# Two residual blocks, deformable stage: VectorE makes four of the nine products of hats per pair, GpSimd keeps five

## What is computed

```python
out = relu(group_norm(conv(x, w1), ...))                 # 1024 -> 256 channels, 1x1
om = conv(out, w_off, pad=1) + b_off                     # 27 channels: 9 x-offsets, 9 y-offsets, 9 masks
off_x, off_y, mask = om[:, :9], om[:, 9:18], sigmoid(om[:, 18:])
py, px = grid_y + ky + off_y, grid_x + kx + off_x        # a place for every pixel and tap
sampled = bilinear_sample(out, py, px) * mask            # 9 taps per pixel
out = einsum('bckhw,ock->bohw', sampled, w2)             # the deformed 3x3 convolution, 256 -> 256
out = relu(group_norm(out, ...))
out = group_norm(conv(out, w3), ...)                     # 256 -> 1024, 1x1
return relu(out + x)
```

## Time and profile before

| | us |
|---|---|
| median of 3 runs | 2977.31 |
| lowest and highest of them | 2972.14, 2982.18 |
| the profiled execution's own time | 2978.64 |
| its span, first to last instruction | 2976.6 |
| PE busy | 2915.8 (98%) |
| DVE busy | 2397.4 (81%) |
| ACT busy | 1795.9 (60%) |
| POOL busy | 712.0 (24%) |

### The profile page before, as it was taken

How to read it: one execution, slowest core, us unless ns; L and a number is a source line. 1 busy time by engine, 2 the same in 40 slices (tenths; PEclk the granted TensorE clock), 3 DMA queues, 4 the chain that set the end, 5 groups by cost and what they waited for, 6 DMA issues and landing times.

```text
span 2976.6 us, 46528 instructions
## 1 busy us (share of the span) xinstructions
PE 2915.8 (98%) x16518; PEld 2864.6 (96%) x16518; DVE 2397.4 (81%) x4872; ACT 1795.9 (60%) x3281; POOL 712.0 (24%) x433
## 2 busy tenths in 40 slices
PE   9999999999998999999999999999999999999997
PEld 9999999999997899999999999999999999999997
DVE  5655888965666688898888988888888888889885
ACT  5544322346664566676666666676776667666664
POOL 0000000000001333333333333333333333333331
PEclk9999999999999999999999999999999999999998
DMA  7774111035653344444444444544444444454431
GB/s 270 218 234 131 44 44 44 22 128 201 262 225 114 122 151 154 152 144 153 152 154 151 143 156 145 163 147 146 159 145 162 146 147 156 149 158 149 147 119 73
DMA packets 209207, 437.39 MB, mean 147 GB/s; under 512 B 18640, under 2 KB 170192, under 8 KB 203344
## 3 DMA queue, kind: packets, MB, share of 16 engines
q1 hardware_dynamic: 159408, 326.82, 32.6%
q10 hardware_dynamic: 49568, 107.60, 11.1%
HBM read 307.71 MB, written 126.64 MB: 146 GB/s over the span
## 4 chain that ended last, share of the span: by engine, by line
PE 56%; DVE 10%; ACT 1%; issue 0%; DMA 0%; POOL 0%; ACTq 0%; SPq 0%; DVEq 0%; POOLq 0%
PE sample L86 6%; PE sample L91 6%; PE deform L86 6%; PE deform L91 6%; PE sample L87 6%; PE deform L87 6%; PE work L86 5%; PE work L91 5%; PE work L87 5%; DVE s_lo L1805 3%; DVE x L1829 2%; DVE x L1711 1%; DVE x_lo L1717 1%; DVE v_lo L1813 1%; PE work L73 1%; PE work L75 1%
## 5 line engine op out<-in xcount | busy, mean ns | idle before, releaser
L1667 POOL TENSOR_TENSOR hats<-hats 98x784 f32<-98x784 f32 x288 | 597.6, 2075 | 909.8 <-DMA hats<-hat_scratch 888.9
L1459 ACT ACTIVATE v_hi<-sample 128x392 fp32r<-128x392 f32 (+1 forms) x640 | 292.2, 463 | 322.5 <-PE sample L91 312.7
L86 PE MATMUL sample<-s_hi,aT_hi 98*128 98x392 f32 (+1 forms) x1280 | 418.1, 332 | 6.4 <-DVE v_lo L1813 6.1
L87 PE MATMUL sample<-s_hi,aT_lo 98*128 98x392 f32 (+1 forms) x1280 | 412.7, 328 | 0.0
L86 PE MATMUL deform<-v_hi,w_w 128*128 128x392 f32 x1152 | 403.7, 350 | 0.0
L87 PE MATMUL deform<-v_hi,w_w 128*128 128x392 f32 x1152 | 393.2, 341 | 0.0
L1813 DVE TENSOR_TENSOR v_lo<-sample,v_hi 128x392 fp32r<-128x392 f32 (+1 forms) x640 | 326.4, 517 | 71.1 <-ACT v_hi L1459 69.9
L1805 DVE TENSOR_TENSOR s_lo<-hats,s_hi 98x784 fp32r<-98x784 f32 x288 | 360.1, 1251 | 2.7 <-ACT s_hi L1450 1.7
L91 PE MATMUL sample<-s_lo,aT_hi 98*128 98x392 f32 (+1 forms) x1280 | 316.4, 328 | 7.1 <-DVE s_lo L1805 7.1
L91 PE MATMUL deform<-v_lo,w_w 128*128 128x392 f32 x1152 | 310.7, 342 | 0.0
L1450 ACT ACTIVATE s_hi<-hats 98x784 fp32r<-98x784 f32 x288 | 245.5, 853 | 105.6 <-DVE x L1711 78.3
(11 more groups left out here) (226 smaller groups left out, 7254.5 us busy)
## 6 DMA issues: line engine op xcount, KB each, us to landing
hats<-hat_scratch SPq DMA_DIRECT2D x768, 150.1 KB
x<-in_x SPq DMA_DIRECT2D x64, 784.0 KB, 5.9
in_home<-y_scratch ACTq DMA_DIRECT2D x248, 196.0 KB, 3.1
out<-x ACTq DMA_DIRECT2D x62, 784.0 KB, 3.4
y_home<-in_x SPq DMA_DIRECT2D x32, 784.0 KB, 4.9
y_scratch<-y_out SPq DMA_DIRECT2D x16, 1568.0 KB, 5.9
terms<-in_x SPq DMA_DIRECT2D x30, 784.0 KB, 4.6
y_scratch<-y_home SPq DMA_DIRECT2D x15, 1568.0 KB, 5.1
```

The costliest lines, as they stand in the source:

```text
L86: nc.tensor.matmul(out, w_hi, x_hi, start=start, stop=False)
L87: nc.tensor.matmul(out, w_lo, x_hi, start=False, stop=False)
L1459: nc.scalar.activation(v_hi[:, group % 2, c, 0:taps_of(g), i, :], sample[:, t % 2, 0:cols(g)].rearrange("p (k s) -> p k s", s=PIX), ACT.Co ...
L1667: nc.gpsimd.tensor_tensor(hats[:, slot, 0:2, 0:n], hats[:, slot, 0:2, 0:n], hats[:, slot, 2:3, 0:n].broadcast_to([HALF, 2, n]), ALU.mult). ...
```

## The change

make_s exists on two engines now. GpSimd makes units 0, 1, 2, 6 and 7 (BY_POOL), VectorE makes units 3, 4, 5 and 8, at places in its own order. Since s_made counts in the order of the units, an engine whose unit follows one of the other engine waits first until that one has been made. Counted from one, as a short name of the change does, VectorE's are units 4, 5, 6 and 9.

```diff
+BY_POOL = (0, 1, 2, 6, 7)
...
+        def loads_until(p, u):
+
+            slot, lap = (UNITS * p.n + u) % HATS, (UNITS * p.n + u) // HATS
+            return 48 * (lap + 1 + (p.n + u // (UNITS - 1) if slot == HATS - 1 else 0))
...
             def make_s(p, u):
                 unit = UNITS * p.n + u
                 n, slot = 2 * PIX, unit % HATS
-                pool.wait_ge(hats_loaded[slot], 48 * (unit // HATS + 1 + (p.n + u // (UNITS - 1) if slot == HATS - 1 else 0)))
+                if u - 1 not in BY_POOL:
+                    at_least(pool, s_made, unit)
+                pool.wait_ge(hats_loaded[slot], loads_until(p, u))
                 nc.gpsimd.tensor_tensor(hats[:, slot, 0:2, 0:n], hats[:, slot, 0:2, 0:n],
                                         hats[:, slot, 2:3, 0:n].broadcast_to([HALF, 2, n]), ALU.mult).then_inc(s_made, 1)
...
                 root(now, gn1)
                 make_s(before, 6)
                 make_s(before, 7)
-                make_s(before, 8)
                 mask_hats(now)
                 root(past, gn3)
                 make_s(now, 0)
                 make_s(now, 1)
                 make_s(now, 2)
-                make_s(now, 3)
-                make_s(now, 4)
                 root(before, gn2)
-                make_s(now, 5)
...
+            @of_pair
+            def make_s(p, u):
+                unit = UNITS * p.n + u
+                n, slot = 2 * PIX, unit % HATS
+                if u - 1 in BY_POOL:
+                    dve.wait_ge(s_made, unit)
+                dve.wait_ge(hats_loaded[slot], loads_until(p, u))
+                nc.vector.tensor_tensor(hats[:, slot, 0:2, 0:n], hats[:, slot, 0:2, 0:n],
+                                        hats[:, slot, 2:3, 0:n].broadcast_to([HALF, 2, n]), ALU.mult).then_inc(s_made, 1)
...
             def second(now, after, coming):
...
                 rest_s(now, 1)
+                make_s(now, 3)
                 rest_v(now, 0)
...
             def step(past, before, now, after, coming):
...
                 rest_x1(after, 3)
+                make_s(now, 3)
                 add_x1(past, 6)
                 add_x1(past, 7)
                 add_y(after, 5)
                 rest_x1(after, 4)
                 rest_v(now, 2)
                 rest_s(now, 2)
+                make_s(now, 4)
                 rest_v(now, 3)
...
                 rest_s(now, 3)
+                make_s(now, 5)
                 rest_b(before)
...
                 rest_s(now, 7)
+                make_s(now, 8)
                 count_y(before, 7)
                 reduce_y(before)
```

## The result

The changed kernel takes 2961.78 us (median of 6 runs, 2957.63 to 2964.16), the kernel before in the same comparison 2977.94 us (6 runs, 2972.14 to 2982.18). The ratio is 0.9944, with a 95% interval of 0.9932 to 0.9956: faster, by 16 us. 2964 was predicted, from 2954 to 2974. The profiled execution took 2961.04 us, its span is 2958.8.

What follows compares the result with a forecast made beforehand. TensorE, busy 1792.62 of 1806 us, was taken as the bound, so only its waits could shrink. The terms -19 + 3 + 4 - 1 = -13 us took the profiled 2978.6 to 2965.6, median 2964, range 2954 to 2974.

Steps and rivals of the forecast that it cites:

- The waits at tile 4 and group_y: Steady pairs: TensorE's waits for s_lo at tile 4 and for the last norm's reduce at group_y go, -19 us.
- The ceiling of 22: Steady pairs: removing waits alone can gain at most 22 us, 0.72 us per pair for some 30 pairs.
- The new waits for loads: Steady pairs, tile 5: VectorE waits for unit 4's load, so v_lo of tile 3 comes late; +3 us, bounds 0 and +9.
- The first pair: First pair, tile 2: v_lo of tile 0 stands behind unit 3's product, which waits for its load; +4 us once.
- Later blocks in this pair fall away as well: First pair: GpSimd's later blocks of VectorE vanish too, reducing the +4 us cost to its lower bound of +2.
- The last pair: Last pair: b_lo on the chain no longer stands behind unit 5's product on GpSimd; -1 us.
- VectorE's load: Steady stretch: four added products per pair are offset by removed blocks, so VectorE's busy share stays about 88%.
- GpSimd's release: Relieving GpSimd of four products gains nothing, since it idles 546 us of 1200 before its products anyway.
- The blocks move: Rival: GpSimd's remaining products hold other VectorE instructions and half the gain is given back; 2974 us, chance 0.24.
- VectorE comes late: Rival: load waits at units 3 and 4 hold v_lo of tiles 2 and 3, +39 for +3; 3000 us, chance 0.08.
- All of it: Rival: no waits for loads show and the first pair gives back half; -21 us, 2956 us, chance 0.15.

Runs made afterwards that it cites:

- e1: Changed kernel with units 3 and 5 back on GpSimd, so VectorE makes only units 4 and 8; 2966.11 us, ratio to the kernel before 0.9967.
- e3: Changed kernel with units 3, 4 and 5 back on GpSimd, so VectorE makes only unit 8; 2966.51 us, ratio to the kernel before 0.9969.
- e4: Changed kernel with units 3, 5 and 8 back on GpSimd, so VectorE makes only unit 4; 2975.05 us, ratio to the kernel before 0.9996.
- e2: Changed kernel with units 4 and 8 back on GpSimd, so VectorE makes only units 3 and 5; 2970.45 us, ratio to the kernel before 0.9984.
- e5: Kernel before, GpSimd making all nine products, but unit 4's product also waits until s_lo of unit 2 is done; 2964.72 us, ratio 0.9962.
- e10: Kernel before, but unit 4's product waits for s_lo of unit 2 and, from the second pair, unit 8's for the last reduce's second instruction; 2964.81 us.
- e7: Changed kernel with units 0, 1, 2, 6 and 7 moved too, so VectorE makes all nine products; 2983.02 us, ratio to the kernel before 1.0019.
- e8: Changed kernel with unit 4's product behind v_lo of tile 3 and, in the first pair, unit 3's behind s_lo of unit 2; 2953.79 us, ratio to before 0.9923.

## Why the prediction was right

The steps, as the prediction put them, against the profiled executions:

- **The waits at tile 4 and group_y, -19.** Right in place and cause (e1, e3 and e4 show each holder by itself; e2 shows that a shift does as well at tile 4), too small in size. 30 clean pairs would take 1844.4 us (29 of 61.52, the mean of the two lengths 61.45 and 61.59 that undisturbed pairs show, and the last one, which has less work, 60.37). Before lost 23.7 us against that, the changed kernel 3.2. In the changed kernel 3.0 of the 3.2 are new, so -23.5 stands where -19 was taken. Counted from tile to tile, before lost 12.1 us at tiles 4 and 5, 7.8 at group_y and 2.8 about tile 0, where s_lo of unit 0 is held, by unit 2 for the most part. The first two make 19.9, near the 19 taken. The 2.8 are a third place that no term has: the prediction named it, in a rival, where it might get worse; it got better (held in 7 of 30 pairs before, in 1 after). The ceiling of 22 was 1.7 low because it took 61.61 us, read off one pair by mask_hats, for a clean pair, where the mean is 61.52. At group_y the prediction named both meetings, unit 8 and mask_hats, for the pair that it read, and the count over all pairs bears it out.
- **The new waits for loads, +3.** +3.0, right in size: five waits of up to 0.4 us shown at tile 5, and six pairs that lose 0.3 to 0.6 from start to start. In the pair shown the load had landed; it is the product's own 0.9 us that is late, more than the wait for the load.
- **The first pair, +4.** +1.0, inside a chance that can be larger (e5 and e10, above). The stall itself was there (3.6 us) and was dearer than thought, by the 1.5 us of half clock behind it; the step that failed is that nothing would be given back. "Later blocks in this pair fall away as well" was its lower bound of +2, and unit 8's block at tile 12 with the half clock behind it was worth 3.2.
- **The last pair, -1.** -0.4: b_lo is off the chain (0.98 us, no wait of PE for it, 1.4 us before), but tile 5 of that pair waits 0.88 us for v_lo behind a product that waited for its load. The other profile of the changed kernel has an end 1.1 us shorter, so a term of this size can't be told from chance.
- **VectorE's load, flat.** Right: 87.4%, products of 0.97 us, no block among them. s_lo's mean fell to 0.974, further than the 1.1 said.
- **GpSimd's release, nothing.** Right: 2.15 us each for what is left, with 464 us of idle time ahead of them.

The errors (-4.5, 0, -3.0, +0.6) sum to -6.9; the +2.3 ahead of the layer leaves -4.6 between the profiled executions, 2965.6 forecast and 2961.0 measured. The medians lie closer, 2964.0 and 2961.8, because the profiled execution lay 1.3 above the median before and 0.7 below it after. That closeness is in part luck: the steady gain was taken too small and the cost of the first pair too large, and the 2.3 us ahead of the layer and the place of the profiled executions among the runs hid much of it. **The blocks move** (2974) was half right as a mechanism: with less than the whole change the loss does move (e4 to the reduce, e10 to v_lo behind unit 3 and to s_lo of unit 0), but with units 3, 4, 5 and 8 all gone from GpSimd little is left at the places where TensorE waits. **VectorE comes late** (3000) did not come true: 0.1 us is lost per pair, its point was 0.55. The nearest to it is e7, with five more products on VectorE: 0.6 us per pair over a clean one, though there by the products' own places and not by waits for loads, which held it up once, ahead of the first pair. **All of it** (2956) fell short only by the two places that e8 cures.

The rule that the prediction took from the Trainium skill (SBUF — State Buffer, "Who interferes with whom"), an exclusive lock between VectorE and GpSimd by order of start, agrees with e5: there the product of unit 4 can only start behind s_lo, no wait for s_lo is left, s_lo of unit 2 is held in none of 30 pairs (15 before), and the time falls by 12.5 us with no work moved.

## What to carry to other kernels

A short meeting of two engines is cheap or dear by what stands behind it in order (s_lo of unit 7 was held in 28 of 29 pairs and cost time in 7); find the two or three meetings that the bound engine waits for, and treat those. Making one engine wait (e5: one semaphore wait, -12.5 us) can do most of what moving the work does, and a moved instruction must not stand ahead of a value that the bound engine wants next (e8 against the changed kernel: -7.0 us for the same instructions at other places). Curing one wait can leave time to be lost at the next one: a part of a cure can measure as nothing (e4, though e5 cures the same wait and gains), so a part that shows no gain alone isn't yet shown to be useless. And a single profile of a short stretch with stalls, as the first pair, can be several us off.

## What the hardware showed that was not expected

TensorE's granted clock fell from 2.4 to 1.2 GHz after 3.60 us of idleness (972.62 in the changed kernel) and also after 2.52 us (996.50 in the kernel before), in both cases over a microsecond after work had begun again, and stayed low for some 3.3 us: matmuls 0.33 us apart in place of 0.18, 1.5 us lost each time. After the wait of 0.86 us at 1001.32 the next matmuls came 0.18 us apart. But in both kernels a longer stretch at 1.2 GHz, some 6.8 us, also comes with shorter waits near each other in the first pair: 1.24, 1.12 and 0.92 us before (978.0 to 981.9), 0.20, 1.12 and 1.00 us in the changed kernel (984.3 to 988.1); that one the change leaves as it was. The Trainium skill, TensorE: Matmul & The Clock Gate, "What's actually happening", says that the clock depends on how busy the engine has been of late; the trace agrees. So a stall of some microseconds costs more than the stall, and one taken away gives back more. It also makes the length of the first pair uncertain: with the same code, e5 had 10 us at 1.2 GHz in it (granted clock 0.91 from 964.90 to 1019.70) and e10 under 1 us (1.00 from 966.90 to 1014.60).
